# Recurrent block on one core: the smallest scan size as a token-pair sum on VectorE, four mixes at once on four row groups, and a slot table of 16 in a new order

## What is computed

```python
# 32 heads of 16; per sequence, over 128 tokens
sx = previous token of xa - xa                      # xa: layer norm of x
h  = tanh((xa + sx*maa_x) @ maa_w1)                 # 5 groups of 32 features
xk, xw, xv, xr, xg = (xa + sx*(maa_stack[j] + h[j] @ maa_w2[j]) for j in range(5))   # the mixes m0..m4
w = exp(-exp(time_decay + tanh(xw @ td_w1) @ td_w2))
r, k, v, g = xr @ Wr.T, xk @ Wk.T, xv @ Wv.T, silu(xg @ Wg.T)
for t in tokens:                                    # state s: 16 x 16 per head
    a = outer(k_t, v_t)
    out_t = r_t @ (u*a + s)
    s = a + w_t[:, None]*s
x1 = x + (group_norm(out)*g) @ Wo.T
x_out = x1 + sigmoid(xr2 @ Wfr.T) * (square(relu(xk2 @ Wfk.T)) @ Wfv.T)
```

## Time and profile before

| | |
|---|---|
| three runs | 4286.19, 4292.06, 4291.24 us |
| median | 4291.24 us |
| the profiled execution, first to last instruction | 4293.0 us |
| mean granted TensorE clock | 0.979 of full |
| TensorE busy | 95% of the span |
| VectorE, ScalarE, GpSimd busy | 54%, 35%, 33% |

### The profile page before, as it was taken

One profiled execution on the slowest core, in us unless ns is written; L12 is line 12 of the kernel. 1 busy time (PEld: TensorE's weight loads), 2 busy tenths in 40 slices (PEclk: granted clock), 3 DMA queues, 4 the chain that ended last, 5 costly groups with the idle time before them and its releaser, 6 DMA issues. The chain is left out here.

```text
span 4293.0 us, 80239 instructions
## 1 busy us (share of the span) xinstructions
PE 4063.9 (95%) x31072; PEld 2552.2 (59%) x31072; DVE 2301.4 (54%) x2657; ACT 1503.0 (35%) x2622; POOL 1419.2 (33%) x1181
## 2 busy tenths in 40 slices
PE   6999999997999999999999999997999999999998
PEld 5666666664666666666666666654445545445443
DVE  3666666663367676666667766325434434434420
ACT  2555555553233344333343333211212222222220
POOL 2343333332254455544445544202211211211210
PEclk9999999998999999999999999998999999999999
DMA  3222222213210010000000001123010110110100
GB/s 109 70 78 65 77 70 77 78 51 106 98 70 26 27 37 26 27 26 27 26 26 26 29 29 62 72 76 149 10 40 0 40 40 0 41 40 0 41 10 10
DMA packets 121024, 205.22 MB, mean 48 GB/s; under 512 B 18784, under 2 KB 39264, under 8 KB 119200
## 3 DMA queue, kind: packets, MB, share of 16 engines
q1 hardware_dynamic: 120736, 200.80, 13.6%
HBM read 125.24 MB, written 67.11 MB: 45 GB/s over the span
## 5 line engine op out<-in xcount | busy, mean ns | idle before, releaser
L1626 DVE COPY_PREDICATED b_A<-b_mask,b_pS 128x2048 f32<-128x2048 uint32 x128 | 458.6, 3582 | 193.9 <-PE b_pS L1313 192.9
L2079 PE MATMUL c_pR<-c_proj_w,c_fcT 128*128 128x512 f32 x1024 | 460.0, 597 | 7.2 <-PEq L1926 3.2
L2019 PE MATMUL c_pR<-s_Wfr,c_fc_w 128*128 128x512 f32 x1024 | 458.4, 598 | 6.4 <-issue 2.3
L718 POOL TENSOR_TENSOR a_S<-a_S,a_negmax 128x2048 f32<-128x2048 f32 x64 | 231.1, 3611 | 489.8 <-DVE a_negmax L652 489.8
L1790 POOL TENSOR_TENSOR b_R<-b_R,b_Wh 128x512 f32<-128x512 f32 x192 | 228.1, 1188 | 394.1 <-PE b_pS L1313 393.8
L2019 PEld LDWEIGHTS c_pR<-s_Wfr,c_fc_w 128*128 128x128 f32 x1024 | 192.2, 191 | 245.5 <-issue 240.9
L2079 PEld LDWEIGHTS c_pR<-c_proj_w,c_fcT 128*128 128x128 f32 x1024 | 189.2, 190 | 235.3 <-issue 224.1
L1313 PE MATMUL b_pS<-b_R,b_kT 32*128 32x128 f32 x7168 | 265.3, 284 | 42.5 <-ACT b_A L1473 30.6
L1313 PEld LDWEIGHTS b_pS<-b_R,b_kT 32*128 32x128 f32 x7168 | 222.7, 186 | 137.8 <-issue 102.5
L2190 DVE TENSOR_TENSOR c_res<-c_res,c_pR 128x512 f32<-128x512 f32 x128 | 88.1, 688 | 402.2 <-PE c_pR L2079 377.3
L2089 ACT ACTIVATE c_fcT<-c_pR,s_vec 128x512 f32<-128x512 f32 x128 | 88.0, 688 | 609.5 <-PE c_pR L2019 580.7
(11 more groups left out here) (257 smaller groups left out, 7911.6 us busy)
## 6 DMA issues: line engine op xcount, KB each, us to landing
a_c<-ctx SPq DMA_DIRECT2D x16, 512.0 KB, 4.0
a_x<-x SPq DMA_DIRECT2D x16, 512.0 KB, 5.0
a_kexp<-a_kT SPq DMA_DIRECT2D x512, 16.0 KB, 1.8
mid_cT<-a_cT SPq DMA_DIRECT2D x16, 512.0 KB, 2.7
a_xl<-x SPq DMA_DIRECT2D x32, 256.0 KB, 2.8
a_cl<-ctx SPq DMA_DIRECT2D x32, 256.0 KB, 3.0
mid_x<-a_xl SPq DMA_DIRECT2D x32, 256.0 KB, 3.3
mid_wy<-a_wy SPq DMA_DIRECT2D x32, 256.0 KB, 2.1
```

Of the source, the lines that this page charges most:

```text
L718: nc.gpsimd.tensor_tensor(S[n % 2][:, :, :], S[n % 2][:, :, :], negmax[n % 2][:, :].unsqueeze(2).to_broadcast([P, RH, T]), ALU.add)\
L1626: nc.vector.copy_predicated(A[:, :, :].rearrange("p q (n two h) -> p q n two h", two=2, h=h)[:, :, :, 1, :], masks[h][:, :].bitcast(U32).r ...
L2019: mm = nc.tensor.matmul(bank, w[:, c, at * P:at * P + P], src[:, c, :], start=(c == 0), stop=(c == KC - 1))
L2079: mm = nc.tensor.matmul(bank, fcT[part % 2][:, m, g * T:g * T + T], proj_w[:, KC * part + m, :], start=(m == 0), stop=(m == KC - 1))
```

## The change

The scan size h = 1 is no longer scored by matmuls. `SCORED` has the sizes 2 to 64, so a sequence has 8 scan steps and a turn 16. GpSimd's products for h = 1 stay, but move to the step `first` of the turn before (and for the second sequence to the PRODUCT step of the first). The pair of neighbouring tokens is put in as follows. VectorE makes `rk1` = (r of the odd token) * (k of the even one); step `u` sums it over each head with 4 more matmuls of 128 columns; `usum` keeps both sums. ScalarE's queue issues a DMA that copies the even tokens' values one partition down into `v_last`. VectorE multiplies `v_last` by the second sum and adds it to `o`: two more TENSOR_TENSOR in each TURNED step.

The steps a0, a1, b0, b1 become a0 and a1 with four mixes each: 8 matmuls on four row groups into all four banks of the ring. For that there are four `xm` tiles; `wT`, `v_pad`, `usum` have one buffer instead of two, and `uT` shares `hid`. GpSimd's additions for m3 and m2 get steps of their own (sum3, sum2). `SLOTS_OF` has 16 lists in a new order. The semaphores of `phase_a` are allocated in another way and cleared inside `phase_norm`.

```diff
+    SCORED = LEVELS[1:]
-    SLOTS = len(LEVELS) + 2
+    SLOTS = len(SCORED) + 2
-    PAIRS = {"a": ("m0", "m1"), "b": ("m2", "m3")}
+    MIXES = ("m0", "m1", "m2", "m3")
+    SUMMED = [("m0", 0), ("m1", 0), ("m0", 1), ("m1", 1), ("m3", 0), ("m3", 1), ("m2", 0), ("m2", 1), ("m4", 0), ("m4", 1)]
     SLOTS_OF = [
-        [("e", "fv0"), ("l", "v0x"), ("p", "x2")],
-        [("e", "fv1"), ("l", "v0y"), ("l", "u"), ("p", "stats")],
-        [("l", "v1"), ("l", "ut"), ("p", "whiten")],
-        [("p", "n1"), ("l", "g0x"), ("f", "gn_mean")],
-        [("p", "shift"), ("l", "g0y"), ("f", "gn_var"), ("l", "g1x")],
-        [("p", "h"), ("f", "gn_div")],
-        [("l", "g1y"), ("p", "a0")],
-        [("p", "a1")],
-        [("f", "gate"), ("p", "k0x")],
-        [("f", "o0"), ("p", "k0y")],
-        [("p", "td"), ("f", "o1")],
-        [("p", "w"), ("f", "stats"), ("p", "k1x")],
-        [("p", "k1y"), ("f", "whiten"), ("p", "b0")],
-        [("p", "b0 sum"), ("f", "n2"), ("p", "b1")],
-        [("p", "m4"), ("f", "shift"), ("p", "r0")],
-        [("p", "r1"), ("f", "fk0")],
-        [("p", "uk"), ("f", "fk1")],
-        [("p", "first"), ("f", "fr0"), ("f", "fr1")],
+        [("e", "fv0"), ("p", "x2")],
+        [("e", "fv1"), ("p", "stats"), ("l", "v0x")],
+        [("l", "u"), ("l", "v0y"), ("l", "ut"), ("p", "whiten")],
+        [("p", "n1"), ("l", "g0x"), ("f", "gn_mean"), ("p", "shift"), ("l", "v1")],
+        [("f", "gn_var"), ("f", "gn_div"), ("l", "g0y"), ("l", "g1x"), ("l", "g1y")],
+        [("p", "h"), ("f", "gate")],
+        [("p", "a0")],
+        [("f", "o0"), ("p", "a1")],
+        [("f", "o1"), ("p", "td"), ("p", "sum3")],
+        [("f", "stats"), ("p", "k0x"), ("p", "k0y")],
+        [("f", "whiten"), ("p", "w"), ("p", "k1x")],
+        [("p", "k1y"), ("p", "sum2"), ("f", "n2")],
+        [("p", "m4"), ("p", "r0")],
+        [("p", "r1"), ("p", "first")],
+        [("f", "shift"), ("f", "fk0"), ("f", "fr0"), ("p", "uk")],
+        [("f", "fk1"), ("f", "fr1")],
     ]
...
     # TensorE, step u
                     for c in range(KC):
-                        mm = nc.tensor.matmul(bank[32 * c:32 * c + 32, 0:TOK], heads_wide[:, :], ruk[:, c, :], start=True, stop=True, skip_group_check=True)
+                        nc.tensor.matmul(bank[32 * c:32 * c + 32, 0:TOK], heads_wide[:, HC:], ruk[:, c, :], start=True, stop=False, skip_group_check=True)
+                    for c in range(KC):
+                        mm = nc.tensor.matmul(bank[32 * c:32 * c + 32, 0:TOK].rearrange("p (n two) -> p n two", two=2)[:, :, 1], heads_wide[:, 0:32], rk1[:, c, :],
+                                              start=False, stop=True, skip_group_check=True)
...
     # ScalarE, step v
+                    act.wait_ge(*R_.out(i, "v", g))
+                    nc.scalar.dma_start(v_last[1:P:2, g, :, :].rearrange("p n z -> p (n z)"), v_pad[0:P:2, g, :, :].rearrange("p n z -> p (n z)")).then_inc(*v_moved[g].up(16))
...
     # VectorE, step uk, and TURNED
+                    nc.vector.tensor_tensor(rk1[:, :, :], odd[:, :, :, 1], even[:, :, :, 0], ALU.mult)
...
+                    nc.vector.tensor_tensor(own, of_heads(v_pad), sums(0), ALU.mult).then_inc(*own_ready.up())
+                    dve.wait_ge(*v_moved[g](i, 16))
+                    nc.vector.tensor_tensor(of_heads(v_last), of_heads(v_last), sums(1), ALU.mult).then_inc(*last_ready.up())
                     dve.wait_ge(*own_ready(i, g + 1))
+                    dve.wait_ge(*last_ready(i, 2 * g + 1))
+                    nc.vector.tensor_tensor(own, own, of_heads(v_last), ALU.add).then_inc(*last_ready.up())
+                    dve.wait_ge(*last_ready(i, 2 * g + 2))
                     dve.wait_ge(*S_.full(i, "s", g, k))
                     nc.vector.tensor_tensor(o[:, g, :], o[:, g, :], pS[:, 1, :], ALU.add).then_inc(*S_.emptied["dve"].up())
...
     # GpSimd
+                elif s == "first":
+                    pool.wait_ge(*decay_ready.all(i))
+                    pool.wait_ge(*ruk_ready(i, 1))
+                    pool.wait_ge(*r_split(i, 1))
+                    move_r(0, 1)
+                    for g in range(G):
+                        move_k(par, g, 1)
+                    pair_totals(i)
```

More of the change, by code:

```diff
@@ L779, in fills @@
         name = {"gate": "gn"}.get(step, step)
-        if step[-1] == "x" or step in ("b0 sum", "x2", "stats", "whiten", "shift", "uk", "first") or step[:3] == "gn_":
+        if step[-1] == "x" or step in ("sum3", "sum2", "x2", "stats", "whiten", "shift", "uk", "first") or step[:3] == "gn_":
             return []
-        if name[0] in PAIRS:
-            return [((m, int(name[1])), "dve") for m in PAIRS[name[0]]]
+        if name[0] == "a":
+            return [((m, int(name[1])), "dve") for m in MIXES]
         name = name.rstrip("y")
@@ L824, in phase_b @@
     unit_at = {(turn, name): (side, n) for side in range(2) for n, (turn, name, who, unit) in enumerate(sides[side])}
-    s_items = [(("s", g, k), "dve" if k == TURNED or k in SCORES and LEVELS[k] < RECT else "act") for g in range(G) for k in range(SLOTS)]
+    s_items = [(("s", g, k), "dve" if k == TURNED or k in SCORES and SCORED[k] < RECT else "act") for g in range(G) for k in range(SLOTS)]
     with ExitStack() as ctx:
@@ L853, in phase_b @@
         sx = [sb("sx0", [P, KC, TOK]), sb("sx1", [P, KC, TOK])]
[L854 to L860 removed]
+        xm = [sb("xm%d" % j, [P, KC, TOK]) for j in range(4)]
+        xm = [xm[0], xm[1], xm[2], xm[3], xm[1]]
+        hid = uT = sb("hid", [P, TOK])
+        kT, gT = (pair(n, [P, KC, TOK]) for n in ("kT", "gT"))
+        rT, wT, rk1 = sb("rT", [P, KC, TOK]), sb("wT", [P, KC, TOK]), sb("rk1", [P, KC, TOK // 2])
+        v_pad, v_last = (sb(n, [P, G, NH // 2, 3 * HD]) for n in ("v_pad", "v_last"))
+        usum, s0 = sb("usum", [P, G, 2, NH]), pair("s0", [P, KC, G, HD])
         R, A = sb("R", [P, 2, KC, T]), sb("A", [P, NH, T])
@@ L900, in phase_b @@
         r_joined, s0_spread = sig("r_joined", G), sig("s0_spread", G)
-        own_ready = sig("own", G)
+        own_ready, last_ready, v_moved = sig("own", G), sig("last", 2 * G), [sig("v_moved%d" % g, 16) for g in range(G)]
         gn_centred, gn_squared, gn_var, gn_root, gn_ready = (sig("gn" + n, 1) for n in ("c", "s", "v", "r", "o"))
@@ L1242, in project @@
                     mm.then_inc(*R_.filled.up())
-                elif s[0] in PAIRS:
+                elif s[0] == "a":
                     h = int(s[1])
-                    banks = [fill(pe, R_, pR, i, m, h, moved=[("h", 0)]) for m in PAIRS[s[0]]]
+                    banks = [fill(pe, R_, pR, i, m, h, moved=[("h", 0)]) for m in MIXES]
                     for m in range(2):
                         at = (2 * h + m) * P
-                        for name, bank in zip(PAIRS[s[0]], banks):
+                        for name, bank in zip(MIXES, banks):
                             rows = slice(int(name[1]) * DM, int(name[1]) * DM + DM)
@@ L1528, in _ @@
             nc.vector.memset(A[:, :, :], 0.0).then_inc(*consts.up())
-            for tile in v_pad:
+            for tile in (v_pad, v_last):
                 nc.vector.memset(tile[:, :, :, :], 0.0).then_inc(*consts.up())
@@ L1596, in project @@
                     ins.then_inc(*R_.emptied["dve"].up(G))
-                elif s[0] in PAIRS:
-                    for name, h in [(m, int(s[1])) for m in PAIRS[s[0]]]:
-                        j = int(name[1])
+                elif s[0] == "a":
+                    h = int(s[1])
+                    if h == 0 and (i + -1).exists():
+                        dve.wait_ge(*R_.full(i + -1, "v", 1))
+                        dve.wait_ge(*R_.full(i + -1, "g", 1))
+                    for j, name in enumerate(MIXES):
                         bank = take(dve, R_, pR, i, name, h)
@@ L1739, in project @@
                     deviation(i, 0)
-                elif s[0] in PAIRS and s != "b0" or s == "m4":
-                    for name, h in [("m4", 0), ("m4", 1)] if s == "m4" else [(m, int(s[1])) for m in PAIRS[s[0]]]:
+                elif s in ("a0", "a1", "sum3", "sum2", "m4"):
+                    for name, h in {"a0": SUMMED[0:2], "a1": SUMMED[2:4], "sum3": SUMMED[4:6], "sum2": SUMMED[6:8], "m4": SUMMED[8:10]}[s]:
                         j = int(name[1])
```

143 lines of the change are left out of this document (74 added, 69 removed).

## The result

The changed kernel takes **4250.82 us** (median of 4 runs, 4247.83 to 4252.37); the kernel before took 4288.72 us beside it (its three runs and a fourth). The ratio is 0.9915, 95% interval 0.9895 to 0.9936: faster by 38 us, 0.85%. The forecast was 4276 us, 15 us less than before. Direction and the range of 4240 to 4312 held; the likeliest case's own range (4268 to 4284) did not, and the gain is two and a half times the one forecast. The profiled execution's span fell from 4293.0 to 4250.3 us.

The account below looks back on a forecast made before the run. TensorE, busy 95% of the span, bounds the kernel. Work 91.0 + waits 8.85 + clock 0.9 give a turn of 100.75 us against 101.49; 13 turns -9.6 and ends -6 give 4276 us, range 4240 to 4312.

Parts of the forecast that it names:

- the likeliest case: The forecast of 4276 us and near it, 4268 to 4284 us; chance 0.34.
- The waits: TensorE's waits a turn: 0.5 + 3.6 (ahead of a1) + 2.55 + 1.64 + 0.55 = 8.85 us, against 5.31 before.
- TensorE's work: Busy work a turn falls from 94.67 to 91.0 us: scores -2.24, mixes -1.72, step `u` +0.3.
- the small waits elsewhere: Slots 10 to 12 come out level and GpSimd costs some tenths as now: 0.55 us a turn in all.
- mixes m0 to m3: Four old mix steps of 0.99 us (3.96) become two of 1.12 (2.24): 1.72 us a turn saved, bounds 0 and 1.98.
- The clock: Clock falls to the 1.2 GHz level behind the wait at a1 in most turns, hardly at m4: +0.9 us a turn.
- Rival C: Low clock lasts from a1 to the end of td: turn 104.15 us, whole 4320 us; chance 0.21.
- Rival A: Clock stays up at the wait ahead of a1: turn 99.85 us, whole 4264 us; chance 0.18.
- The ends: Turns outside the 13 inner ones: 11 us of removed work, about half taken for the same waits, so -6 us.
- What was costed at nothing: GpSimd's h = 1 products, `rk1`, the two DMAs, single buffers and clearing `phase_a`'s semaphores (0 to 2 us): taken as 0.
- Rival B: VectorE's TURNED products take 0.68 us each, clock up: wait at a1 2.3, turn 98.55, whole 4247 us; chance 0.11.
- B's far end: The two long waits shrink to 1.2 us and nothing: turn 94.4 us, whole 4193 us.

Follow-up runs that it names:

- pair_early: Changed kernel with VectorE's three products of the first sequence's TURNED step moved ahead of the mixes of a0: 4209.05 us, ratio 0.9826, turn 96.10 us.
- two_by_two: Changed kernel with the mixes issued two at a time again instead of four: 4283.23 us, ratio 0.9993, turn 100.74 us.

## Why the forecast had the right sign and too small a size

**The waits: right.** A turn whose clock fall costs nothing takes 98.28 us. TensorE is busy 91.15 us of it [window above], and 1.50 of these are the lower clock at the score and o1 (0.30 and 1.20 beyond their full-clock lengths). That leaves 89.65 of work and 8.63 of waits, where the prediction had 8.85. Its places, owners and order held. Two of its numbers missed in opposite directions: the products took 3.99 us instead of 3.33, so that from a0 to a1 it was 9.72 and not 9.3; and the small waits elsewhere came to 0.35 instead of 0.55.

**TensorE's work: the step that failed by size.** The prediction had the busy work fall from 94.67 to 91.0 us; it fell to 89.65. Added up over the timelines of two clean turns, from each group's start to the next one's less the waits:

| us a turn | before | after, full clock | difference | forecast |
|---|---|---|---|---|
| score steps | 15.61 | 13.16 | -2.45 | -2.24 |
| mixes m0 to m3 | 4.24 | 2.05 | -2.19 | -1.72 |
| u | 0.57 | 0.79 | +0.22 | +0.3 |
| g and k, now in fewer pieces (7 groups, now 5) | 15.17 | 14.52 | -0.65 | 0 |
| all else | 59.23 | 59.13 | -0.10 | 0 |
| sum | 94.82 | 89.65 | -5.17 | -3.66 |

(Counted from start to start the kernel before has 94.82 us, 0.15 more than by the window.) A half of a g or k step behind a score costs 1.92 us, one behind other 128-row work 1.73 to 1.83, and a whole one in one piece behind a score 3.66. So an order that cuts these steps less often, or sets them behind other 128-row work, saves TensorE 0.1 to 0.2 us at each seam; I took the order as free. That the seams are the cause is read from these lengths, no run tested it. For the mixes I took one old step at its shortest place (0.99) where the four came to 4.24, and gave a new one 1.12 where a0 took 1.08 and a1 0.97.

**The clock: mechanism right, size near.** The fall came at a1 or right behind it in every turn (most turns were forecast), and none at m4. It cost 0.95 us where it reached a1 and nothing where it began behind it: 0.71 on average (98.99 - 98.28), against +0.9. Rival C, low clock through td, did not happen: td took 1.09 us. Rival A's condition, a clock that stays up, did not hold in any turn, though the whole came out beyond its 4264: through the work, not through the clock.

**The sum.** 100.75 forecast, 98.99 measured: -1.35 by TensorE's work, -0.22 by the waits, -0.19 by the clock. Thirteen turns are 22.9 us. The ends gave -10.2 against -6, of which 5.6 are the earlier start of `phase_b` told above. What was costed at nothing stayed hidden: no wait of TensorE names the DMAs into `v_last`, and TensorE is idle 9.48 us ahead of the first matmul of `phase_b`, before 9.29, so clearing the semaphores costs at most 0.2 us.

**Rival B** (VectorE less late with products at 0.68, and the clock up) was wrong for this kernel: the products took 3.99 us and the wait ahead of a1 was 3.93, not 2.3. That the whole, 4250.82, lies nearer to its 4247 than to the 4276 is chance. pair_early goes further than B, as it takes the products out of the chain altogether: 96.10 us a turn, where B had 98.55. (B's far end is misadded: waits of 1.2 us and nothing make a turn of 94.9, not 94.4, and so 4200 us, not 4193.)

The Trainium skill (SBUF — State Buffer, section SBUF: two separate sides) says that VectorE and GpSimd share a port pair that one of them holds for a whole instruction, while the other is blocked, and that a VectorE operation with two SBUF inputs takes part in it against a GpSimd operation that reads SBUF. The trace agrees: the products take 1.66 and 1.55 us beside GpSimd's additions, 0.68 without them, while the additions go from 1.16 to 1.6 each. From the first addition's start (2064.90) to the last product's end (2068.66) it is 3.76 us, and the four take 2.32 + 1.36 = 3.68 us without each other, as if they took turns.

## What to carry to other kernels

When two engines hand each other work through a few buffers, look for what the work that you take off the busier one had covered. In this kernel taking out the same two score steps cost 0.74 us a turn in one order and gave 2.22 after an exchange of two list entries. Work through the late engine's queue between a buffer's filling and its release, and pull out of it whatever doesn't need to stand there; three short products moved by one step gave more (2.9 us a turn) than the whole change (2.5). And sum a step's cost over all its places in the turn, not from its best one, seams between groups included.

## What the runs showed of the hardware

- A fall of the clock costs what it delays, not what it stretches: here a fall cost 0 or 0.95 us a turn, by whether it reached the one step that VectorE was waiting for. Filling the gap with matmuls of 3.62 us kept the clock up there and moved the fall to the next gap, where it cost up to 3.6 us.
- Three TENSOR_TENSOR of 128x512 float32 took 3.99 us, two of them beside GpSimd's additions, and 2.05 alone.
- COPY_PREDICATED of 128x2048 elements takes 4.75 us or so at h = 2 and 2.36 to 2.40 at h = 4 and 8, the same number of elements: the path of this kernel hangs on the first of them twice a turn.
- Four mixes on four row groups, 16 instructions of 256 columns, took 1.08 us at a0, and 8 such instructions on two row groups 1.07 at the same place (two_by_two): four row groups do twice the columns in the same time. (At a1 the 16 took 0.97, and the 8 at their best 0.99 in the earlier trace rows.)
